# Adaptive-norm attention and mixture-of-experts layer: last head scores, early routing and GpSimd's mixing buffer rearranged in the drain

## The reference

```
y   = clip(modulated_linear(x))                        # 128 -> 128
x1  = x + y + attention(y)                             # 4 groups x 4 heads, key width 64
kx  = modulated_linear2(x1)                            # 128 -> 128
scores = einsum('nhd,njd->nhj', kx, kx) / sqrt(8)      # per token: 16 heads of 8 features
mix = einsum('nhj,njd->nhd', softmax(scores), kx)      # "mixing": heads of one token mix
tok = modulated_linear3(mix)
```

```
probs = softmax(tok @ gate_w.T); two best experts per token
keep  = experts chosen at most 640 times
out   = x1 + sum_e gate[t, e] * (relu(tok @ W1[e] + b1[e]) @ W2[e] + b2[e])
```

## Time and profile before

| | |
|---|---|
| median of 3 runs | 661.29 us (660.55 to 661.64) |
| the profiled execution | 660.68 us, of which 658.9 us is the span of the trace |
| TensorE matmul busy | 622.5 us (94%) |
| VectorE busy | 521.1 us (79%) |
| ScalarE busy | 413.2 us (63%) |
| GpSimd busy | 288.1 us (44%) |

### The profile page before, as it was taken

One profiled execution on the slowest core, in us unless ns is written; L12 is line 12 of the kernel. 1 busy time (PEld: TensorE's weight loads), 2 busy tenths in 40 slices (PEclk: granted clock), 3 DMA queues, 4 the chain that ended last, 5 costly groups with the idle time before them and its releaser, 6 DMA issues. The chain is left out here.

```text
span 658.9 us, 15267 instructions
## 1 busy us (share of the span) xinstructions
PE 622.5 (94%) x4388; PEld 506.5 (77%) x4420; DVE 521.1 (79%) x1155; ACT 413.2 (63%) x823; POOL 288.1 (44%) x251
## 2 busy tenths in 40 slices
PE   8899999999999999999999999999999996889998
PEld 8687778787878787878787878787878786756665
DVE  6246888888888888888888888888888879877766
ACT  2776767777676767777777777777777541334343
POOL 5122555555555555555555555555555457000000
PEclk9999999999999999999999999999999999899999
DMA  7200000000000000000000000000000000000004
GB/s 244 50 1 1 1 2 1 0 0 0 0 0 0 0 0 0 0 0 0 0 0 0 0 0 0 0 0 0 0 0 1 2 0 1 1 0 1 0 0 127
DMA packets 9364, 7.18 MB, mean 11 GB/s; under 512 B 1089, under 2 KB 8833, under 8 KB 9217
## 3 DMA queue, kind: packets, MB, share of 16 engines
q1 hardware_dynamic: 9344, 6.94, 3.6%
HBM read 4.84 MB, written 2.10 MB: 11 GB/s over the span
## 5 line engine op out<-in xcount | busy, mean ns | idle before, releaser
L1092 POOL TENSOR_TENSOR pair<-kx 128x1152 f32<-128x1152 f32 x32 | 82.4, 2574 | 164.1 <-ACT kx L836 159.8
L611 PEld LDWEIGHTS bank_a<-v,prob 128*128 128x128 f32 x1024 | 127.0, 192 | 17.0 <-issue 15.8
L603 PE MATMUL bank_t<-qT,k_one 128*128 128x512 f32 x256 | 130.7, 592 | 6.1 <-POOL neg_diag L1084 4.7
L611 PE MATMUL bank_a<-v,prob 128*128 128x65 f32 x1024 | 131.8, 272 | 0.0
L295 DVE TENSOR_REDUCE row_max<-bank_s 128x4 f32<-128x512 f32 x128 | 87.3, 682 | 13.3 <-PE bank_s L594 8.9
L836 ACT ACTIVATE prob<-bank_t 128x512 f32<-128x512 f32 x128 | 76.3, 596 | 29.6 <-PE bank_t L603 26.4
L440 DVE CAST k<-k_one 64x512 bf16<-64x512 f32 x32 | 50.1, 1565 | 54.3 <-ACT k_one L836 54.3
L1072 POOL TENSOR_TENSOR mix_hi<-mix_hi 128x512 f32<-128x512 f32 (+2 forms) x96 | 80.2, 835 | 7.5
L1084 POOL TENSOR_TENSOR neg_diag<-neg_max,own_w 16x512 bf16<-16x512 f32 x32 | 36.3, 1135 | 95.9 <-ACT neg_max L836 83.1
L836 ACT ACTIVATE qT<-misc 64x512 f32<-64x512 f32 x128 | 75.5, 590 | 4.0 <-PE misc L618 1.6
L618 PEld LDWEIGHTS misc<-yT,wq_sb 128*128 128x128 f32 x512 | 64.5, 192 | 15.9 <-issue 14.9
(11 more groups left out here) (155 smaller groups left out, 1103.3 us busy)
## 6 DMA issues: line engine op xcount, KB each, us to landing
out<-acc_all SPq DMA_DIRECT2D x8, 256.0 KB, 2.3
x_all<-in_xT SPq DMA_DIRECT2D x1, 1024.0 KB, 9.0
w_sb<-in_w SPq DMA_DIRECT2D x2, 512.0 KB
x_all<-in_xT SPq DMA_DIRECT2D x1, 768.0 KB, 6.9
wq_sb<-in_wq SPq DMA_DIRECT2D x1, 512.0 KB, 4.5
wpost_sb<-in_wpost SPq DMA_DIRECT2D x1, 512.0 KB, 9.8
x_all<-in_xT SPq DMA_DIRECT2D x1, 256.0 KB, 3.6
b_rows<-in_b SPq DMA_DIRECT2D x16, 4.0 KB
```

Source lines behind the costliest of these rows:

```text
L603: mm(bank_t[g % 2][:, :, :], k_one[:, j, g, :], qT[:, j, HPG * g:HPG * (g + 1), :], start=False, stop=True).then_inc(s_t_mm, 1)
L611: last = mm(att_bank(g)[:, w, :], prob[:, g % 2, w, :], v1[:, j, g, :], start=(w == 0), stop=True, skip_group_check=True)
L1092: G.tensor_tensor(pair[:, :, :], bass.AP(kx2, jc * 2 * P, [[4 * P, P], [0, SHIFTS], [1, P]]), bass.AP(kx2, jc * 2 * P, [[4 * P, P], [MD, S ...
```

## The change

Four edits. In slots 33 and 34 VectorE does the head scores ahead of the whole mixing and no longer in the middle of it. `first_choice(EARLY)` moves from the end of slot 33 to slot 34, behind `mix` 31, where `second_choice(EARLY)` follows. ScalarE's `route_exp(EARLY)` moves from slot 33, ahead of `mixT` 30, to slot 34, behind `mixT` 31. `mix_hi` gets two buffers, and GpSimd's product waits for the sum of the batch before the last. In the slots up to 32 VectorE's order is the same as before. The unchanged lines of the mixing are only moved down in the text.

```diff
-        mix_hi = sb("mix_hi", [P, MH // 2, P])
+        mix_hi = sb("mix_hi", [P, 2, MH // 2, P])
...
+                if late(s):
+                    head_scores()
                 if D:
                     dve.wait_ge(s_weight, n(d))
                     need(dve, s_mix, n(d - 1))
                     V.tensor_tensor(mix_lo[:, :, :].rearrange("p r (h e) -> p r h e", e=MD),
...
                     V.tensor_tensor(mix_lo[:, 0, :], mix_lo[:, 0, :], mix_lo[:, 1, :], ALU.add).then_inc(s_lo, 1)
-                if late(s):
-                    head_scores()
-                    mixed()
-                    if s == BATCH + 2:
-                        second_choice(EARLY, 1)
-                else:
-                    mixed()
+                mixed()
+                if not late(s):
                     head_scores()
-                if s_is(s, BATCH + 1):
+                if s_is(s, BATCH + 2):
                     dve.wait_ge(s_log, 1)
                     dve.wait_ge(s_const, 3)
                     first_choice(EARLY)
+                    second_choice(EARLY, 1)
...
                 if late(s):
                     head_weights()
-                if s_is(s, BATCH + 1):
-                    route_exp(EARLY)
...
                     f(mixT[:, :], misc[2][:, 0, :], scale=style[:, 2, bass.ds(d, 1)]).then_inc(s_mixT, 1)
+                if s_is(s, BATCH + 2):
+                    route_exp(EARLY)
...
                     pool.wait_ge(s_weight, n(d))
-                    need(pool, s_msum, n(d - 1))
+                    need(pool, s_msum, n(d - 2))
```

More of the change, by code:

```diff
@@ L361, in slot @@
                     V.tensor_tensor(x_all[:, col(a)], x_all[:, col(a)], yT[:, :], ALU.add).then_inc(s_xy, 1)
[L362 to L384, removed]
                 def mixed():
@@ L388, in mixed @@
                         dve.wait_ge(s_hi, 4 * d + 4)
-                        V.tensor_tensor(mix_sum[:, :], mix_lo[:, 0, :], mix_hi[:, 0, :], ALU.add).then_inc(s_msum, 1)
+                        V.tensor_tensor(mix_sum[:, :], mix_lo[:, 0, :], mix_hi[:, jd, 0, :], ALU.add).then_inc(s_msum, 1)
                         dve.wait_ge(s_hrden, n(d))
@@ L426, in slot @@
                     head_scores()
-                    mixed()
-                    if s == BATCH + 2:
-                        second_choice(EARLY, 1)
-                else:
-                    mixed()
+                if D:
+                    dve.wait_ge(s_weight, n(d))
+                    need(dve, s_mix, n(d - 1))
+                    V.tensor_tensor(mix_lo[:, :, :].rearrange("p r (h e) -> p r h e", e=MD),
+                                    weight[:, jd, 0:MH // 2, :].unsqueeze(3).to_broadcast([P, MH // 2, MH, MD]),
+                                    bass.AP(kx2, jd * 2 * P, [[4 * P, P], [MD, MH // 2], [MD, MH], [1, MD]]),
+                                    ALU.mult).then_inc(s_lo, 1)
+                if D:
+                    V.tensor_reduce(h_den[:, :], weight[:, jd, :, :].rearrange("p r h -> p h r"), AX.X,
+                                    ALU.add).then_inc(s_hden, 1)
+                    dve.wait_ge(s_lo, 4 * d + 1)
+                    V.tensor_tensor(mix_lo[:, 0:4, :], mix_lo[:, 0:4, :], mix_lo[:, 4:8, :], ALU.add).then_inc(s_lo, 1)
+                if C:
+                    dve.wait_ge(s_post_mm, n(c))
+                    dve.wait_ge(s_xy, n(c))
+                    V.tensor_tensor(x_all[:, col(c)], misc[2][:, 0, :], x_all[:, col(c)], ALU.add).then_inc(s_x1T, 1)
+                if D:
+                    dve.wait_ge(s_hden, n(d))
+                    V.reciprocal(h_rden[:, :], h_den[:, :]).then_inc(s_hrden, 1)
+                    dve.wait_ge(s_lo, 4 * d + 2)
+                    V.tensor_tensor(mix_lo[:, 0:2, :], mix_lo[:, 0:2, :], mix_lo[:, 2:4, :], ALU.add).then_inc(s_lo, 1)
+                    dve.wait_ge(s_lo, 4 * d + 3)
+                    V.tensor_tensor(mix_lo[:, 0, :], mix_lo[:, 0, :], mix_lo[:, 1, :], ALU.add).then_inc(s_lo, 1)
+                mixed()
+                if not late(s):
                     head_scores()
-                if s_is(s, BATCH + 1):
+                if s_is(s, BATCH + 2):
                     dve.wait_ge(s_log, 1)
@@ L1063, in slot @@
                     pool.wait_ge(s_weight, n(d))
-                    need(pool, s_msum, n(d - 1))
-                    G.tensor_tensor(mix_hi[:, :, :].rearrange("p r (h e) -> p r h e", e=MD),
+                    need(pool, s_msum, n(d - 2))
+                    G.tensor_tensor(mix_hi[:, jd, :, :].rearrange("p r (h e) -> p r h e", e=MD),
                                     weight[:, jd, MH // 2:MH, :].unsqueeze(3).to_broadcast([P, MH // 2, MH, MD]),
@@ L1071, in slot @@
                         pool.wait_ge(s_hi, 4 * d + i + 1)
-                        G.tensor_tensor(mix_hi[:, 0:r, :], mix_hi[:, 0:r, :], mix_hi[:, r:2 * r, :],
+                        G.tensor_tensor(mix_hi[:, jd, 0:r, :], mix_hi[:, jd, 0:r, :], mix_hi[:, jd, r:2 * r, :],
                                         ALU.add).then_inc(s_hi, 1)
```

## The result

The changed kernel takes 665.35 us (median of 6 runs, 664.76 to 665.86) against 661.18 us before (6 runs, 660.55 to 661.65): a ratio of 1.0063, 95% interval 1.0050 to 1.0076. It is 4.2 us slower. The forecast was 662.5 us, with a range that ended at 665.3. The measured time lies beside the middle of the rival "TensorE's clock falls a second time" (665.2). Two further series, on other chips, put the same kernel less far above the one before, 1.7 us (E5, E12).

What follows compares the result with a forecast made beforehand. The chain over TensorE's padding, then VectorE's routing, was taken to bound the drain. A later `first_choice(RECENT)`, +1.25 us less up to 0.15, on the 661.29 us median gave 662.5 us, range 659.5 to 665.3.

Steps and rivals of the forecast that it cites:

- TensorE's clock falls a second time: Rival: longer idle ahead of `count` halves TensorE's clock, +2 to +3.5 us, 664.5 to 666, middle 665.2; chance 0.22.
- The sum: Drain total: `first_choice(RECENT)` starts at about 570.4 instead of 569.14, +1.25 us, less up to 0.15; all else 0.
- the end of TensorE's padding ahead of the transpose of `mix` 31: In the drain, the 12 padding calls were to end where they did before; bounds -1.4 to +0.8 us.
- Turns of VectorE and GpSimd: In mixing 30 and 31, GpSimd's early product takes turns: `mix` 30 at 558.5 instead of 556.67, `mix` 31 at 562.4.
- the 555.2 of the rival: Faster rival: VectorE keeps its turn through mixing 30, `mix` 30 at 555.2, kernel 658.8 us; chance 0.17.
- The 553.9 for engines that did not meet: Time of `mix` 30 if VectorE and GpSimd took no turns; the sum would then be about 655 us.
- The transpose of `mix` 31: On TensorE behind the padding: starts at 566.6, bounds 565.2 to 567.4, though `mix` 31 is ready 2.6 us earlier.
- gate products near 561, and the 12 padding calls end where they did: On TensorE after `mixT` 30: clock again at 0.50, so 24 padding records cost 4.8 us; 2.6 at the higher level.
- The wait for the exponential: VectorE waits some 3 us for ScalarE's early exponential; `second_choice(EARLY)`, 2.93 us long, then lasts to 570.5.
- The clock: Ahead of `count`, TensorE's idle grows from 2.0 to 3.3 us; the forecast case, chance 0.45, counted no second fall.
- The kernel before holds its clock behind 566: Before the change TensorE idled 2.0 us ahead of `count` (570.6 to 572.6) and its clock stayed at 1.00.
- The two buffers in the loop: The second `mix_hi` in the 28 loop slots costs 0, since GpSimd never waited for VectorE's sum there.

Runs made afterwards that it cites:

- E5: The changed kernel again, unaltered, on another chip: 663.82 us, ratio 1.0030 to the kernel before.
- E12: The changed kernel once more, unaltered, in a third series on another chip: 663.69 us, ratio 1.0032 to the kernel before.
- E3: The changed kernel with GpSimd's product waiting for the last batch's sum again, as with one buffer: 661.28 us, ratio 0.9994 to the kernel before.
- E10: The changed kernel with 62 instead of 40 padding calls in slot 33, ahead of the transpose of `mix` 30: 661.21 us, ratio 0.9999 to the kernel before.
- E2: The changed kernel with ScalarE's early exponential ahead of `mixT` 31 instead of behind it: 662.43 us, ratio 1.0011 to the kernel before.
- E7: The kernel before with 8 padding calls in TensorE's 2.0 us gap ahead of `count`: 662.2 us, ratio 0.9996 to the kernel before.
- E8: The kernel before with only the two buffers for GpSimd's half of the mixing: 662.15 us, ratio 1.0003 to the kernel before.
- E4: The kernel before with only ScalarE's early exponential moved behind `tok_all` 30 in slot 33: 660.89 us, ratio 0.9986 to the kernel before.
- E1: The changed kernel with 12 more padding calls in TensorE's gap ahead of `count`: 663.73 us, ratio 1.0035 to the kernel before.
- E9: The changed kernel with 12 padding calls ahead of `count` and 6 behind the first bias rows: 663.73 us, ratio 1.0028 to the kernel before.
- E6: The changed kernel with the edits of E2 and E3 and 10 padding calls ahead of `count`: 660.27 us, ratio 0.9974 to the kernel before.

## Why the prediction was right and wrong

The step that failed is the choice to put the price of TensorE's clock behind the new wait at nothing. The sum held one term, +1.25 us for the later start of `first_choice(RECENT)`; the trace has +2.16 there and another 1.9 to 2.0 for a second fall of the clock. The second step, contained in the +2.16, is the end of TensorE's padding ahead of the transpose of `mix` 31, put at 0 and measured +0.7. The prediction had named its own sign of being wrong, the clock at 0.50 behind 574, and that is what the trace shows. That the rival's middle (665.2) is so close is partly luck: it is 662.5 + 2.7, and the result is made of a larger first term (2.2) and a smaller price of the fall (2.0) than it has.

- *Turns of VectorE and GpSimd:* right. `mix` 30 was worked out at 558.5 and ended at 558.57, `mix` 31 at 562.4 and 562.48. The `shifted` of batch 31 lost its race by the hair foreseen (1.40 us instead of 0.43), the 512-wide add took 2.37. E3 takes GpSimd's early product away and gives the 555.2 of the rival. (The 553.9 for engines that did not meet is not what the rows give; 549.98, 0.48 and some 3.8 make about 554.3. Nothing hangs on it.) The rule of the Trainium skill (SBUF — State Buffer, Who interferes with whom), that the one that comes second is blocked for the whole instruction, agrees with these rows.
- *The transpose of `mix` 31:* placed at 566.6, it came at 567.27, inside its bounds (565.2 to 567.4). This term of the sum was set at 0, with up to 0.15 taken off, and measured +0.7. What failed is "gate products near 561, and the 12 padding calls end where they did". The clock had fallen at about 556.2 instead of 558.7, so the three calls ahead of the product of `mixT` 30 took 1.49 us instead of 0.83; that product came 0.6 later, `tok_all` 30 (560.91) and the gate products (561.42) 0.46 later, and the clock rose 0.9 us later than before. The text had named these three calls and then let them give back only the 0.15. E10 shows the clock as the cause: with it at 1.00 the transpose comes at 564.15.
- *The wait for the exponential:* right in mechanism (3.85 us, expected some 3) and in its price: 568.33 to 571.30 is 2.97, expected 2.93. The start of `first_choice(RECENT)` moved by 2.16 instead of 1.25 us; 0.7 of the difference is the transpose, the rest the handovers around the exponential and 0.1 that the prediction dropped itself (its second choice lasts to 570.5, its first choice of `RECENT` starts at 570.4). E2 shows the wait as a cause.
- *The clock:* the likeliest case assumed that it does not fall a second time, with 0.22 for the rival that it does. It fell in the trace of the result. The gap came out as worked out (3.46 against 3.3 us); the price, put at 2 to 3.5 us, came out at its lower end (1.9 by the rows of `count` and of the output products, against E12). What was wrong is the choice between them: the case was treated as a toss for the kernel, with half the weight of the forecast, and the upper end of the range (665.3) cut off half of that rival's own range. The six times of the result (664.76 to 665.86) all lie with the long executions; on the other chips it was 5 of 16. Why does not come out of the runs: neither the gap nor the program differs, but the chip and the occasion do, and on the occasion of the result the kernel before, too, was 0.7 to 0.9 us faster than in the later series.
- *The kernel before holds its clock behind 566:* right in its own trace; E7 had this gap padded and says nothing of it. The traces of E2 and E8 show that a gap of 2 us can be enough, that of E4 that the one of 1.6 us ahead of the hidden products can (these took 3.66 instead of 1.98). So the lower end of "between the 2.0 that held and the 5.3 that did not" was not a safe one.
- *The two buffers in the loop:* right, E8.

## What to carry to other kernels

An engine's early start is only free if it takes nothing from the engine that is waited for: where two engines take turns at operand reads, give the turn to the one with the longer chain behind it (here one constant in one semaphore wait is worth 3.8 us at the transpose and 2.4 in the median). An instruction moved to another place in a strict queue takes over every wait ahead of it: the exponential moved behind `mixT` inherited TensorE's padding. And a change that lets TensorE idle longer is to be priced with the work that comes after at half clock. Padding pays where the half clock lies on the chain that ends last: in the gap of slot 33 it was worth 2.5 us (E10), in the new gap ahead of `count` nothing in the median (E1, E9), though it may take away the longest executions. If executions fall into groups, look at the granted clock of each stretch in more than one trace before the median.

## What the runs showed of the hardware that was not expected

- One program, with equal waits, can have its clock fall in one execution and not in another: gap of 3.46 us, then 0.50 (profile of the changed kernel, and E5 with 3.45), and 3.45 us, then 1.00 (E12; E3 too, with its one other constant).
- What a second fall costs differs from trace to trace: measured from `count` to the third group of output products 1.9 us in the changed kernel and in E5, 1.7 in E4 and E6, 1.0 in E2 and E10, nothing in E8.
- The times lie in two groups, 2 to 3 us apart (E3: 658.7 to 660.5 and 662.1 to 662.6), and a median of few executions jumps between them. For the changed kernel three traces fit a second fall in the upper group only; the trace of E10, a fall and yet a time of the lower group, does not fit, so the cause of the groups in general stays open.
- It fell behind shorter gaps than was thought: 1.99 us in E2, where it fell 1.2 us after TensorE had resumed, 1.99 us in E8, and 1.56 us in E4.
- The turns passed about 0.14 us before an instruction's end in all chains looked at, so that whole schedules of two engines can be worked out to 0.1 us.
